# A sequence layer and a mixture of experts on one core: the results of the last expert tiles added into the output by indirect transfers instead of gathered and added on chip

## What is computed

```python
x = x + attn(layernorm(x))     # 16 heads of 8: a recurrence over time; its output rows
                               # are spread over N as z, z, o (stack of two zero rows and o, last N rows kept)
x = x + ffn(layernorm(x))      # per token: one of E = 16 experts (argmax of the logits), plus a shared MLP
# ffn: scores = sigmoid(logits) * onehot; y_e = (up * silu(gate)) @ down_proj[e] of scores * x
#      shared = (silu(x @ w_gate.T) * (x @ w_up.T)) @ w_down.T ; out = shared + y_e
```

## Time and profile before

| | us |
|---|---|
| median of the runs | 670.8 (670.62 to 671.29) |
| the profiled execution, its own time | 673.13 |
| its span, first to last instruction | 671.4 |
| mean granted TensorE clock in it | 0.917 of full |
| busy: TensorE matmul / VectorE / POOL / ScalarE | 528.3 / 492.5 / 360.0 / 248.9 |

### The profile page before, as it was taken

How to read it: one execution, slowest core, us unless ns; L and a number is a source line. 1 busy time by engine, 2 the same in 40 slices (tenths; PEclk the granted TensorE clock), 3 DMA queues, 4 the chain that set the end, 5 groups by cost and what they waited for, 6 DMA issues and landing times.

```text
span 671.4 us, 7382 instructions
## 1 busy us (share of the span) xinstructions
PE 528.3 (79%) x1809; PEld 273.7 (41%) x1810; DVE 492.5 (73%) x809; ACT 248.9 (37%) x515; POOL 360.0 (54%) x349
## 2 busy tenths in 40 slices
PE   1768989999999886877387689879999967578930
PEld 1434434444454433322154455525454255345520
DVE  3369999989898998799589999498999775412201
ACT  1825754444445242111122145533545124135520
POOL 4235767666667575654567333366767574700023
PEclk9868999999999998887799799998999977979985
DMA  9601116700000590000611012300100021112224
GB/s 218 138 0 32 32 42 162 217 0 1 0 1 0 141 356 35 1 0 0 170 35 55 17 48 69 110 15 16 31 23 18 0 52 35 43 56 63 63 80 111
DMA packets 46706, 41.79 MB, mean 62 GB/s; under 512 B 4588, under 2 KB 40248, under 8 KB 46168
## 3 DMA queue, kind: packets, MB, share of 16 engines
q1 hardware_dynamic: 43140, 35.61, 18.9%
q0 software_dynamic: 2400, 5.38, 2.7%
q10 hardware_dynamic: 1136, 0.46, 0.3%
HBM read 23.80 MB, written 17.63 MB: 62 GB/s over the span
## 4 chain that ended last, share of the span: by engine, by line
DVE 33%; PE 30%; issue 16%; POOL 12%; DMA 5%; ACT 2%; ACTq 1%; POOLq 0%; DVEq 0%; SPq 0%
DVE grown L1412 9%; PE ps L1874 6%; DVE early L1527 5%; POOL grown L1062 4%; DVE ps L1451 4%; PE ps L1831 4%; PE ps L1891 3%; DVE early L1532 3%; PE ps L1832 2%; PE ps L1931 2%; DVE grown L1439 2%; POOL uv L978 2%; PE ps L1639 2%; DVE grown L1405 2%; POOL early L1009 2%
## 5 line engine op out<-in xcount | busy, mean ns | idle before, releaser
L1062 POOL TENSOR_TENSOR grown<-grown 128x512 f32<-128x512 f32 x64 | 80.8, 1272 | 101.4 <-DVE grown L1439 101.4
L1412 DVE TENSOR_TENSOR grown<-ps,steps 128x1536 f32<-128x1536 f32 x64 | 112.1, 1752 | 1.8
L1831 PE MATMUL ps<-grown,cst 128*128 128x512 f32 x128 | 77.7, 692 | 27.8 <-DVE grown L1412 27.6
L857 ACT ACTIVATE uv<-ps 128x512 f32<-128x512 f32 x64 | 38.1, 597 | 110.5 <-DVE grown L1439 110.5
L1874 PE MATMUL ps<-steps 128*128 x128 | 69.6, 642 | 8.8 <-issue 8.6
L1832 PE MATMUL ps<-grown,cst 128*128 128x512 f32 x128 | 71.4, 641 | 0.0
L978 POOL TENSOR_TENSOR uv<-uv,steps 128x512 f32<-128x512 f32 x64 | 67.7, 1081 | 1.7 <-ACT uv L857 1.6
L1310 DVE TENSOR_TENSOR e_h<-rk,ps 128x256 f32<-128x256 f32 x64 | 25.4, 417 | 53.8 <-ACT rk L870 34.0
L1839 PE MATMUL ps<-uv,cst 128*128 128x512 f32 x128 | 60.4, 594 | 0.4 <-POOL uv L978 0.4
L1117 POOL TENSOR_TENSOR early<-state,qT 128x512 f32 x22 | 37.2, 1690 | 32.4 <-DVE state L1426 32.4
L1088 POOL COPY early<-early 128x32 f32<-128x32 f32 x63 | 27.5, 436 | 43.9 <-DVE early L1532 43.9
(11 more groups left out here) (221 smaller groups left out, 1001.8 us busy)
## 6 DMA issues: line engine op xcount, KB each, us to landing
steps<-gate_up_proj SPq DMA_DIRECT2D x1, 4096.0 KB, 15.3
xs_others<-zeros SPq DMA_DIRECT2D x1, 2496.0 KB, 10.9
steps<-xs_others SPq DMA_DIRECT2D x19, 128.0 KB, 2.1
ys_others<-e_y SPq DMA_DIRECT2D x19, 128.0 KB, 1.9
early<-chain_m SPq DMA_DIRECT2D x4, 512.0 KB, 6.3
xf<-x SPq DMA_DIRECT2D x4, 495.0 KB
normed<-early SPq DMA_DIRECT2D x28, 64.0 KB, 1.7
xs_mixed<-zeros SPq DMA_DIRECT2D x1, 1728.0 KB, 8.9
```

What stands on the lines that cost most here:

```text
L1062: G.tensor_tensor(decayed[:, h], decayed[:, h], work[:, h, 1], ALU.add).then_inc(s_add[h], 1)
L1412: V.tensor_tensor(grown[:, :, h].rearrange("p e (x w) -> p e x w", w=HD), st, per_col(tile, FF, 3, h, HD), ALU.mult).then_inc(s_prod[h], 1)
L1831: T.matmul(bank[2 * h + 1], c["block"], work[:, h, 1], start=True, stop=True).then_inc(s_usum[h], 1)
```

## The change

Expert results of the mixed tokens no longer go through `ys_mixed`. Each row of the slot table gets a 129th number, the row number of its token in `out`; the table is a new tensor `slots` with rows of 516 bytes. Rows of `out` are stored from `xf` once, complete but for the mixed tokens' expert part, by 12 transfers of ScalarE ahead of its pairs. POOL waits for them, and then, for every pair, copies the pair's 2 x 128 row numbers to integers (`tokens`, on POOL) and adds the two tiles of e_y into `out` by two indirect transfers with an add (`compute_op=ALU.add`). Empty slots carry row numbers of the others (`idle_mixed`, set at the start by a transfer of 4-byte elements), distinct within a tile, and add zeros there. Gone are the 13 stores of pairs, the 11 gathers, the two adds of VectorE, and the 36 stores of `out` at the end. `over_pairs` writes the first two pairs of the mixed run out and so loops over 8 pairs instead of 10.

```diff
+def tokens_of(t):
+
+    tok = 3 * L2 * (np.arange(P)[:, None] % C) - 3 * SKIP + np.asarray(t.rows)[None, :]
+    return np.where((tok >= 0) & (tok < N), N * (np.arange(P)[:, None] // C) + tok, 0)
+
+
 def constants():
...
         assert (~v).sum() <= P
+    parts["token_mixed"] = tokens_of(MIXED)
+    at_rest = (P * np.arange(MIXED.tiles + 1)[None, :] + p[:, None]) % (2 * B * (N // 3))
+    within = at_rest % (2 * (N // 3))
+    parts["idle_mixed"] = N * (at_rest // (2 * (N // 3))) + 3 * (within // 2) + within % 2 + 1
     parts["prefer"] = np.tile(E - np.arange(E)[None, :], (P, 1))
...
         normed = nc.dram_tensor("normed", (B, N, D), F32).ap()
+        slots = nc.dram_tensor("slot_rows", ((MIXED.tiles + 1) * P, D + 1), F32).ap()
+        out_rows = out.rearrange("b n d -> (b n) d")
...
             else:
-                rows, scaled = take(t.n * D), take(t.n * D)
+                rows, scaled = take(t.n * D), take(t.n * (D + 1))
                 q["rows"] = q["shared"] = [rows[:, j * D:(j + 1) * D] for j in range(t.n)]
-                q["scaled"] = [scaled[:, j * D:(j + 1) * D] for j in range(t.n)]
-                q["back"] = rows
+                q["sent"] = [scaled[:, j * (D + 1):(j + 1) * (D + 1)] for j in range(t.n)]
+                q["scaled"] = [r[:, 0:D] for r in q["sent"]]
+                q["token"] = scaled.rearrange("p (n d) -> p n d", d=D + 1)[:, :, D]
                 q["lg"] = take(t.n * E)
...
         left = steps[:].rearrange("p a b c -> p (a b c)")[:, E * 3 * F:L1 * 5 * P]
-        assert 4 * U * P <= left.shape[1]
-        e_in, e_xT = (left[:, k * 2 * U * P:(k + 1) * 2 * U * P].rearrange("p (b u d) -> p b u d", b=2, u=U)
-                      for k in (0, 1))
+        assert 2 * U * (P + D + 1) <= left.shape[1]
+        e_row = left[:, 0:2 * U * (D + 1)].rearrange("p (b u d) -> p b u d", b=2, u=U)
+        e_in = e_row[:, :, :, 0:D]
+        e_xT = left[:, 2 * U * (D + 1):2 * U * (P + D + 1)].rearrange("p (b u d) -> p b u d", b=2, u=U)
+        e_to = sb("e_to", [P, 2, U], I32)
         e_y = sb("e_y", [P, 2, U, P])
...
                                                 sem("s_e_out"), two("s_e_written"))
-        s_gat, s_fin, s_out = {t: two("s_gathered_" + t) for t in fb}, sem("s_final"), sem("s_out")
-        s_ends = sem("s_out_ends")
+        s_gat, s_fin, s_out = sem("s_gathered"), sem("s_final"), sem("s_out")
+        s_to, s_acc = sem("s_e_tokens"), two("s_e_added")
         SETS = (OTHERS, MIXED)
         GA = {OTHERS.name: 0, MIXED.name: len(OTHERS.groups)}
-        PARTS = ((0, MIXED.n // 2 + 1), (MIXED.n // 2 + 1, MIXED.n))
...
             n = run.n
-            looped = (n - 3) // 2 * 2
-            with engine.Fori(0, looped // 2) as half:
+            alone = 2 if run.t is MIXED else 0
+            looped = alone + (n - 3 - alone) // 2 * 2
+            for k in range(alone):
+                pair(0, k, n - 1 - k)
+            with engine.Fori(alone // 2, looped // 2) as half:
                 i = half * 2
...
         def routed(t):
+            if t is MIXED:
+                return slots.rearrange("(m p) d -> p m d", p=P), None
             return (xs[t.name].rearrange("(m p) d -> p m d", p=P), ys[t.name].rearrange("(m p) d -> p m d", p=P))
-
-        def middle_rows(b):
-
-            n = 3 * SKIP
-            return out[b, ROWS - n:(C - 1) * ROWS - n:3, :].rearrange("(g r) d -> g r d", r=L2)
...
             sp.wait_ge(s_zero, 2)
-            for t in SETS:
-                sp.dma_start(xs[t.name].rearrange("(m p) d -> p m d", p=P),
-                             zeros[:, 0:D].unsqueeze(1).to_broadcast([P, t.tiles + 1, D])).then_inc(s_xz, 16)
-                sp.dma_start(ys[t.name][t.tiles * P:, :], zeros[:, 0:D]).then_inc(s_xz, 16)
+            t = OTHERS
+            sp.dma_start(xs[t.name].rearrange("(m p) d -> p m d", p=P),
+                         zeros[:, 0:D].unsqueeze(1).to_broadcast([P, t.tiles + 1, D])).then_inc(s_xz, 16)
+            sp.dma_start(ys[t.name][t.tiles * P:, :], zeros[:, 0:D]).then_inc(s_xz, 16)
+            rows = slots.rearrange("(m p) d -> p m d", p=P)
+            sp.dma_start(rows[:, :, 0:D], zeros[:, 0:D].unsqueeze(1).to_broadcast([P, MIXED.tiles + 1, D])).then_inc(s_xz, 16)
+            sp.wait_ge(s_cst2, 16)
+            sp.dma_start(rows[:, :, D:], c["idle_mixed"].unsqueeze(2), allow_slow_non_contiguous=True).then_inc(s_xz, 16)
             for r in (0, 1):
...
             sp.wait_ge(s_scat[MIXED.name], 16 * MIXED.n)
-            pairs_in_out(sp, RUNS[2])
-            n = 3 * SKIP
-            last = N - ((C - 1) * ROWS - n)
-            sp.wait_ge(s_fin, 1)
-            for b in range(B):
-                g0 = b * C
-                sp.dma_start(out[b:b + 1, 1:ROWS - n, :], xf[g0:g0 + 1, n + 1:, :]).then_inc(s_out, 16)
-                for q in (1, 2):
-                    sp.dma_start(out[b, ROWS - n + q:(C - 1) * ROWS - n:3, :].rearrange("(g r) d -> g r d", r=L2),
-                                 xf[g0 + 1:g0 + C - 1, q::3, :]).then_inc(s_out, 16)
-                    sp.dma_start(out[b:b + 1, N - last + q:N:3, :],
-                                 xf[g0 + C - 1:g0 + C, q:last:3, :]).then_inc(s_out, 16)
-            for part, (lo, hi) in enumerate(PARTS):
-                sp.wait_ge(s_fin, 2 + part)
-                for b in range(B):
-                    sp.dma_start(middle_rows(b)[:, lo:hi, :], xf[b * C + 1:b * C + C - 1, 3 * lo:3 * hi - 2:3, :]
-                                 ).then_inc(s_out, 16)
-            sp.wait_ge(s_out, 16 * 7 * B)
-            sp.wait_ge(s_ends, 16 * 2 * B)
+            x_in, _ = routed(MIXED)
+            run = RUNS[2]
+            for k in range(run.n):
+                sp.wait_ge(s_et, k + run.g0 - 1 if k >= 2 else run.g0)
+                if k >= 2:
+                    sp.wait_ge(s_to, k - 1)
+                sp.dma_start(e_row[:, k % 2], x_in[:, k * U:(k + 1) * U, :]).then_inc(s_ei[k % 2], 16)
+            sp.wait_ge(s_out, 16 * 3 * B)
+            for k in (0, 1):
+                sp.wait_ge(s_acc[k], 16 * U * ((RUNS[2].n + 1 - k) // 2))
         @block.scalar
...
                 act.wait_ge(s_ey, i + (k + run.g0 + 1))
-                act.wait_ge(s_ew[b], written)
+                if run.t is MIXED:
+                    if type(i) is int and i + k < 2:
+                        act.wait_ge(s_ew[b], 16 * (1 + run.base[b]))
+                    else:
+                        act.wait_ge(s_acc[b], i * (8 * U) + 16 * U * (k // 2))
+                else:
+                    act.wait_ge(s_ew[b], written)
                 S.activation(e_y[:, b], b_y(run).rearrange("p (u d) -> p u d", u=U), ACT.Copy).then_inc(s_eo, 1)
...
             q = fb[MIXED.name]
+            S.activation(q["token"], c["token_mixed"], ACT.Copy).then_inc(s_sc, 1)
             for j in range(MIXED.n):
             shared(MIXED)
-            pairs(RUNS[2])
-
             n = 3 * SKIP
             last = N - ((C - 1) * ROWS - n)
-            act.wait_ge(s_fin, 3)
+            act.wait_ge(s_fin, 1)
+            act.wait_ge(s_fa, GA[MIXED.name] + len(MIXED.groups))
             for b in range(B):
                 g0 = b * C
-                act.dma_start(out[b:b + 1, 0:1, :], xf[g0:g0 + 1, n:n + 1, :]).then_inc(s_ends, 16)
-                act.dma_start(out[b:b + 1, N - last:N:3, :], xf[g0 + C - 1:g0 + C, 0:last:3, :]).then_inc(s_ends, 16)
+                act.dma_start(out[b:b + 1, 0:ROWS - n, :], xf[g0:g0 + 1, n:, :]).then_inc(s_out, 16)
+                act.dma_start(out[b, ROWS - n:(C - 1) * ROWS - n, :].rearrange("(g r) d -> g r d", r=ROWS),
+                              xf[g0 + 1:g0 + C - 1, :, :]).then_inc(s_out, 16)
+                act.dma_start(out[b:b + 1, N - last:, :], xf[g0 + C - 1:g0 + C, 0:last, :]).then_inc(s_out, 16)
+            pairs(RUNS[2])
...
             def scatter_tile(t, j):
-                q = fb[t.name]
-                pool.wait_ge(s_sc, TB[t.name] + j + 1)
-                G.indirect_dma_start(xs[t.name], bass.IndirectOffsetOnAxis(ap=q["idx"][:, j:j + 1].bitcast(U32), axis=0),
-                                     q["scaled"][j], None).then_inc(s_scat[t.name], 16)
+                q, m = fb[t.name], t is MIXED
+                pool.wait_ge(s_sc, TB[t.name] + j + 1 + m)
+                G.indirect_dma_start(slots if m else xs[t.name],
+                                     bass.IndirectOffsetOnAxis(ap=q["idx"][:, j:j + 1].bitcast(U32), axis=0),
+                                     q["sent" if m else "scaled"][j], None).then_inc(s_scat[t.name], 16)
...
                                          bass.IndirectOffsetOnAxis(ap=q["idx"][:, j:j + 1].bitcast(U32), axis=0)
-                                         ).then_inc(s_gat[t.name][int(t is MIXED and j >= PARTS[1][0])], 16)
+                                         ).then_inc(s_gat, 16)
...
             scatter(MIXED)
-            pool.wait_ge(s_fa, GA[MIXED.name] + len(MIXED.groups))
-            m = RUNS[2].n
```

(29 more changed lines are left out.)

## The result

The changed kernel takes 685.48 us (median of 4 runs, 682.96 to 688.41), the kernel before beside it 670.71 (4 runs, 669.66 to 671.29): a ratio of 1.0222, interval 1.0182 to 1.0262. The range held the time; the sign and the 667.5 us are wrong. The profiled execution took 684.19 us with a span of 682.4, which answers to the earlier trace rows. Each later job measured its own runs of the kernel before, so variants are compared by their ratio to that.

A forecast was written before the change was run, and what follows sets the result against it. Bound by the 26.0 us transfer tail after pairs paced by TensorE; start 602.8 + twelve POOL-paced steps 60.8 + last pair and end gave span 668.1, median 667.5 us; whole range 656 to 690, own range 664.9 to 671.4.

The forecast's parts named there:

- the sign: Whole kernel: faster than the one before, chance 0.50 against 0.45 for slower; forecast median 667.5 us against 670.8.
- What bounded the kernel, and what is removed: Kernel's end: the tail after the last y is transfers, not work; all 26.0 us of it is removed.
- a to d: Added slot-table fill, ScalarE's row-number copy, 12 early store issues (some 3.8 us), peeled pairs: all covered or worth nothing.
- The stores' data: Before the pairs: 2048 KB of early stores, not covered, end at 596; first y at 602.0, first adding transfer 602.8.
- The centre, the chain of the pairs: POOL's pairs: each starts only after the previous landed; step 1.0 + 1.27 + 2.8 = 5.07 us, twelve take 60.8 us.
- First to second issue: 0.97 us: Within a pair's step on POOL: issue taken as 0.97 us plus 0.30 between the two, 1.27 us.
- The landing of 2.8: Adding transfer, issue to landing: 2.8 us with read and write overlapped; low end 2.2, high end 4.8.
- rival 2: Adding transfer reads and writes in series: landing 3.8 us, step 6.07, span 681.1, median 680.5; chance 0.33.
- rival 3: Adding transfer's descriptors take twice as long: issue 1.95 us, 2 us more a step, 693; chance 0.12 together with another rival.
- rival 1: Adding transfer lands like a plain scatter, 2.2 us: step 4.47, span 660.3, median 659.7; chance 0.15.
- The rule weighed there: DMA cost is fixed, not by bytes: about 2.15 us for each of a pair's two 64 KB transfers; span 659.7.
- 0.4 to the end of SyncE: Program's end: after the last pair's second issue and landing (1.27 + 2.8), 0.4 us remains to the span's end.

The follow-up runs named there:

- number 6: Changed kernel with row numbers copied by VectorE into each pair's own buffer, no wait for landings: ratio 0.991, repeated on another chip 0.9896.
- Number 4: Changed kernel without the 12 early stores of the output and the waits for them: 678.56 us, ratio 1.0116.
- number 9: Changed kernel, steps kept; wide add waits for scatters, SyncE issues stores behind four loads, first two copies precede POOL's wait for stores: 682.92 us, ratio 1.0187.
- number 7: As number 6, plus VectorE's wide add waiting for all scatters and SyncE issuing the 12 stores behind its first four loads: ratio 0.9839.
- numbers 9 to 11: number 9; then kernel before with only the wide add waiting for all scatters, 670.11 us, ratio 0.9985; then number 7 repeated, 658.64 us, ratio 0.9812.
- number 1: Changed kernel with a buffer per pair for row numbers, so the copy no longer waits for landings: 668.29 us, ratio 0.9948.
- Number 3: Changed kernel with plain scatters, compute_op=ALU.add left out, all waits kept: 667.12 us, ratio 0.9939.

## Why the prediction was wrong

- **What bounded the kernel, and what is removed:** right. The tail was transfers, and nothing of it is left but the last pair's.
- **The start of the kernel (a to d):** right in effect. The zero fill took 13.9 us and not 8.9, and SyncE's next issue came at 219.8: covered. The 12 stores took 7.9 us of ScalarE's queue (581.77 to 589.68) where I said 3.8, but ScalarE's first work was only due at 593.01. That held because the loads were late as well; in number 6 the same issues were not covered.
- **The stores' data:** the mechanism was right, the size off by 3.3 us. POOL was free of the stores' wait at 594.8, where I had 596. But the last scatter, which I left at 4.4 us from start to landing, took 7.0, and the loads of the first two pairs 5.7 and 7.0, where I had taken half of the possible delay (loosely: 7.2 - 2.2 is 5.0 and not 6, and half of that 2.5 and not 3.2). The chain of waits goes through the second of them and not through POOL's wait for the stores; that the loads are the later of the two was predicted rightly. Number 4 puts the whole price of the stores at 6.4 to 7 us, and part of it is avoidable by order alone. How much, no run tells cleanly: number 9 saves 2.9 us together with the shorter scatter, and number 7 saves 3.8 us with the scatter out of play, but there against ScalarE's issues and not against the stores' data. Here is what the Trainium skill, "SBUF — State Buffer", Who interferes with whom, says: a VectorE instruction with two inputs in SBUF contends with a GpSimd instruction that reads SBUF. The trace agrees: 3.12 us beside the wide add, 0.96 and 0.97 in numbers 9 to 11, which keep them apart. The same section ends by saying that such an add did not stall the writing of a DMA's descriptors; for this indirect transfer the measurement is otherwise. The small gates, which I had put at nothing, did nothing: 18 issues in a row took 1547 to 1558 ns.
- **The centre, the chain of the pairs:** the order of waits was read correctly, and number 1 shows that it costs 18 us. The price of a step was wrong: 6.00 instead of 5.07. Release to start was 0.86 (I had 1.00). The failed term is "First to second issue: 0.97 us, between the gather's 0.955 and the scatter's 0.98". The issue of an adding transfer is 1.56. This enters twice, between the issues and in the landing: 2 x 0.59 = 1.18. The landing of 2.8 was otherwise well placed: less its issue it had 1.83 us, measured are 1.74. So 5.07 + 1.18 - 0.14 - 0.09 = 6.02.
- **The rivals:** the time of rival 2 (span 681.1) is near the 682.4, but not for its reason. Read and write in series would have given 3.8 - 0.97 = 2.8 us behind the issue; 1.74 came, 0.5 more than without an add. It is rival 3 that happened, at 0.59 us and not at 0.97, and I had argued it away with two rows of transfers that do not add. Number 3, with the add left out, has the step of rival 1, but not its time: 667.1 and not 659.7 us, since start and end were as late as in the changed kernel.
- **The rule weighed there:** a plain transfer lands after 2.2 us in number 3, close to the estimate of 2.15 us from the Trainium skill, "DMA: Bandwidth & Descriptors", Anatomy of one DMA. Had it held for the adding one, the change would have been faster, by 0.6% as number 3 was. By measurement that one takes 3.3 us, and 0.6 of the 1.1 us more are POOL's issue. The page puts the fixed cost mainly on completion and not on setup; here the issue is 0.96 of the 2.2 us even without the add.
- **The end:** "0.4 to the end of SyncE" failed. SyncE was done at 678.0, but POOL's drain lasted to 682.2. I looked only at SyncE's wait, since in the kernel before it ends last; the drain of 14.7 us stood in that trace, hidden by 3.7 us.
- **The last pair:** its step is 3.74 instead of 6.00, since no copy stands ahead of it; I had missed this in my favour by 2.3 us.

By the prediction's own sum the sign turned at a landing of 3.05 us, and 3.3 came; the issue alone, doubled in its effect, was enough for that, and so was the end, where the span goes on for 4.4 us behind the last landing and not for 0.4: the forecast's span was only 3.3 us shorter than the one before. No row showed an adding transfer, and while I bounded its landing from both sides, I gave its issue a single value inside the sum.

## What to carry to other kernels

A small copy that frees a buffer is a link in two chains: ask both what it waits for and which load waits for it, and put it on an engine that has neither slow transfers ahead of it nor behind it. Moving work from the end into a loop pays only if the loop's new wait is shorter than the loop's own step; count from one landing to the next, with the issue of the transfer taken from a row of the same kind, or with both bounds if there is none. Indirect transfers of POOL should not be the last work of a program if something else can be.

## What the runs showed of the hardware

- An indirect transfer of 128 rows of 512 bytes with an add takes 1.56 us of POOL to issue and lands after 3.3; without the add 0.96 and 2.2. With the add it has 112 packets more (the changed kernel and number 3).
- POOL's drain at the close of the program lasts until 5.6 to 6.9 us after the end of the last indirect transfer's issue (all 14 traces; the 6.9 is number 3), 4.2 us beyond the landing in the changed kernel.
- Small loads issued just behind 2 MB of stores land after 5.7 to 7.0 us instead of 2.2 (the changed kernel and number 4). The Trainium skill, "DMA: Bandwidth & Descriptors", Queues, rings and completion order, has each DMA engine take turns between queues by whole packets; that fits, but no run here varied the packets.
- A wide add of VectorE (128 x 2816 in float32, 3.08 us) stretches a scatter that starts beside it from 0.97 to 3.1 us of issue.
